# The turned tokens of a fused attention and feed-forward kernel: made per token half instead of per block of channels

## The reference, cut to what matters

```python
x = L0_attn_x                                        # (16, 512, 256)
x = _layernorm(x + _L0_attn_ref(x, Wqkv, bqkv, Wout, bout))
x = _layernorm(x + _L0_ffn_ref(x, ...))

def _tlin(x, w, s):
    return jnp.einsum('bsi,oi->bso', x, w) * s
h = jax.nn.silu(_tlin(x, w1_w, w1_s)) * _tlin(x, w2_w, w2_s)     # 256 -> 1024
h = jax.nn.gelu(_tlin(h, h1_w, h1_s), approximate=False)         # 1024 -> 1024
h = jax.nn.gelu(_tlin(h, h2_w, h2_s), approximate=False)         # 1024 -> 1024
return _tlin(h, w3_w, w3_s)                                      # 1024 -> 256
```

## Time and profile before

| | |
|---|---|
| median of three executions | 2168.33 us |
| span of the profiled execution (first to last instruction) | 2166.8 us |
| PE busy | 2118.4 us, 98% |
| ACT busy | 1316.1 us, 61% |
| DVE busy | 1259.9 us, 58% |
| POOL busy | 492.9 us, 23% |
| mean granted PE clock | 0.991 of full speed |

### The profile page before, as it was taken

The page is one execution under the profiler, slowest core; times in us unless marked ns, Lnnn a source line. Parts: engine busy times, 40 slices in busy tenths (PEclk is TensorE's granted clock), DMA queues, the critical chain, the costliest instruction groups (busy, mean ns, idle before and its releaser), DMA issues.

```text
span 2166.8 us, 52048 instructions
## 1 busy us (share of the span) xinstructions
PE 2118.4 (98%) x16294; PEld 1878.8 (87%) x16294; DVE 1259.9 (58%) x3928; ACT 1316.1 (61%) x2807; POOL 492.9 (23%) x899
## 2 busy tenths in 40 slices
PE   8789999999999999999999999999999999999998
PEld 4368889989889888899989889988999898988998
DVE  7765555556555565556556565565556556565452
ACT  6456566666556666566666666666566666656553
POOL 2222122221222222122221122222122132122220
PEclk9889999999999999999999999999999999999999
DMA  8742332232322332332232322333232232321100
GB/s 275 239 120 63 77 71 70 61 81 64 90 65 61 82 74 69 75 69 73 61 81 64 90 64 62 81 76 73 71 76 70 56 82 69 83 64 37 37 6 10
DMA packets 95940, 167.69 MB, mean 77 GB/s; under 512 B 19204, under 2 KB 38404, under 8 KB 95672
## 3 DMA queue, kind: packets, MB, share of 16 engines
q1 hardware_dynamic: 91912, 152.75, 28.6%
q10 hardware_dynamic: 3760, 11.54, 1.5%
HBM read 98.26 MB, written 68.17 MB: 77 GB/s over the span
## 4 chain that ended last, share of the span: by engine, by line
PE 89%; DVE 1%; DMA 0%; issue 0%; SPq 0%; ACT 0%; POOL 0%; POOLq 0%; DVEq 0%
PE ring L1241 44%; PE ring L1226 10%; PE pM L1116 7%; PE pS L1104 6%; PE pO L1164 6%; PE ring L1254 5%; PE ring L1176 4%; PE ring L1206 2%; PE ring L1196 2%; PE ring L1148 1%; PE ring L1215 1%; DMA qk_d<-c 0%; SPq L614 0%; DVE full_g L960 0%; DMA Qs<-nm 0%
## 5 line engine op out<-in xcount | busy, mean ns | idle before, releaser
L921 DVE CUSTOM_DVE_ANT_0 pM<-pM,mask 128x512 f32<-128x512 f32 (+3 forms) x1024 | 498.7, 502 | 366.1 <-PE pM L1116 292.3
L1241 PE MATMUL ring<-Yhi,H 128*128 128x256 f32 x1984 | 501.7, 289 | 0.0
L1241 PE MATMUL ring<-Xhi,H 128*128 128x256 f32 x1984 | 497.9, 288 | 0.0
L1241 PE MATMUL ring<-Ylo,H 128*128 128x256 f32 x1984 | 489.2, 282 | 0.0
L1241 PE MATMUL ring<-Xlo,H 128*128 128x256 f32 x1984 | 486.4, 282 | 0.0
L1241 PEld LDWEIGHTS ring<-Ylo,H 128*128 128x128 f32 x1984 | 377.8, 190 | 7.2 <-issue 3.4
L1241 PEld LDWEIGHTS ring<-Yhi,H 128*128 128x128 f32 x1984 | 377.0, 190 | 7.1 <-issue 3.4
L1241 PEld LDWEIGHTS ring<-Xlo,H 128*128 128x128 f32 x1984 | 379.1, 191 | 0.8
L1241 PEld LDWEIGHTS ring<-Xhi,H 128*128 128x128 f32 x1984 | 378.4, 191 | 1.0 <-issue 0.2
L1116 PE MATMUL pM<-Ks,Qs 128*128 128x512 f32 x992 | 304.2, 340 | 20.6 <-DVE mx L921 9.0
L865 ACT ACTIVATE Yhi<-ring,cols 128x256 fp32r<-128x256 f32 x248 | 117.8, 475 | 266.8 <-PE ring L1241 170.1
(11 more groups left out here) (146 smaller groups left out, 3518.7 us busy)
## 6 DMA issues: line engine op xcount, KB each, us to landing
qk_d<-c SPq DMA_DIRECT2D x120, 256.0 KB, 3.4
Qs<-qk_d SPq DMA_DIRECT2D x120, 192.0 KB
Ks<-qk_d SPq DMA_DIRECT2D x120, 192.0 KB
qk_d<-c SPq DMA_DIRECT2D x120, 128.0 KB, 3.0
xTs<-in_xT SPq DMA_DIRECT2D x16, 512.0 KB, 4.3
raw<-in_h SPq DMA_DIRECT2D x8, 1024.0 KB, 10.4
xz<-in_x SPq DMA_DIRECT2D x16, 512.0 KB, 3.9
H<-raw ACTq DMA_DIRECT2D x8, 1024.0 KB, 9.3
```

The lines of the kernel that those rows point to most:

```text
L921: nc.vector.tensor_tensor_reduce(pM[:, h % 2, 0:n], pM[:, h % 2, 0:n], mask[:, T - n:T], 1.0, NEG, ALU.add, ALU.max, mx[:, t, h:h + 1]).th ...
L1241: mm = nc.tensor.matmul(to, w, x_part, start=(k == 0 and m == 0), stop=(k == KB - 1 and m == 1))
```

## The change

A turn now makes one token half for both channel blocks: the argument of `x1_turn` is the half. The four transposes go into one bank as (channel block, token), ACT copies the whole bank into an `x1Thi` of half the size, and DVE fills an `x1Tlo` of half the size. The second half's turn overwrites the first half's buffers, so ACT waits until the first half's gate and up products have read them, and the turn stands behind them: in `ORDER` and `FIRST_ORDER` ahead of `ffn_out:-1:0:0`, in `TAIL_ORDER` right ahead of `gu:-1:1:0`, and in `HEAD_ORDER` no longer at all. The freed space is held by a placeholder tensor, so all other addresses stay.

```diff
-ffn_out:-2:1:0 x1_turn:-1:1 exp:0:1:0 exp:0:1:1 ffn_out:-2:1:1 exp:0:1:2 max:0:2:3:2 exp:0:1:3 gu:-1:0:0
+ffn_out:-2:1:0 exp:0:1:0 exp:0:1:1 ffn_out:-2:1:1 exp:0:1:2 max:0:2:3:2 exp:0:1:3 gu:-1:0:0
...
-h2:-1:0:7:1 max:1:0:3:0 qk:1:1 ffn_out:-1:0:0 table:0:Exp:6 exp:0:3:0 max:1:0:3:1 exp:0:3:1 stack:1:1
+h2:-1:0:7:1 max:1:0:3:0 qk:1:1 x1_turn:-1:1 ffn_out:-1:0:0 table:0:Exp:6 exp:0:3:0 max:1:0:3:1 exp:0:3:1 stack:1:1
...
-ffn_hi:-1:0:5 gu:-1:0:7 ffn_hi:-1:0:6 gu:-1:1:0 ffn_hi:-1:0:7 gu:-1:1:1 ffn_hi:-1:1:0 gu:-1:1:2 ffn_hi:-1:1:1
+ffn_hi:-1:0:5 gu:-1:0:7 ffn_hi:-1:0:6 x1_turn:-1:1 gu:-1:1:0 ffn_hi:-1:0:7 gu:-1:1:1 ffn_hi:-1:1:0 gu:-1:1:2 ffn_hi:-1:1:1
...
-        x1Thi = sb("x1Thi", [P, CB, T], F32R)
-        x1Tlo = sb("x1Tlo", [P, CB, T], F32R)
+        x1Thi = sb("x1Thi", [P, CB, HALF], F32R)
+        x1Tlo = sb("x1Tlo", [P, CB, HALF], F32R)
+        ctx.enter_context(nc.sbuf_tensor("x1_room", [P, CB, T], F32))
...
-                        c, = a
-                        act.wait_ge(xt_ready, b * CB + c + 1)
+                        half, = a
+                        act.wait_ge(xt_ready, b * 2 + half + 1)
...
-                        need(act, gu_ready, b * (2 * KB))
-                        nc.scalar.activation(x1Thi[:, c], ring[:, BANKS[kind, off, a]], ACT.Copy).then_inc(x1_hi, 1)
+                        need(act, gu_ready, b * (2 * KB) + half * KB)
+                        nc.scalar.activation(x1Thi[:].rearrange("p c n -> p (c n)"), ring[:, BANKS[kind, off, a]], ACT.Copy).then_inc(x1_hi, 1)
...
-                        for t in range(TB):
-                            mm = nc.tensor.transpose(to[:, t * P:(t + 1) * P], xz[:, (odd + off) % 2, t, c * P:(c + 1) * P], ident[:].bitcast(F32))
+                        for c in range(CB):
+                            for t in range(2):
+                                at = c * HALF + t * P
+                                mm = nc.tensor.transpose(to[:, at:at + P], xz[:, (odd + off) % 2, 2 * half + t, c * P:(c + 1) * P],
+                                                         ident[:].bitcast(F32))
...
-                        pe.wait_ge(x1_lo, (b + 1) * CB)
-                        tok = slice(half * HALF, (half + 1) * HALF)
+                        pe.wait_ge(x1_lo, b * 2 + half + 1)
```

More of the change, by code:

```diff
@@ L129 @@
 max:1:1:0:2 max:1:1:0:3 weights:0:10 pv:1:0:1 neg_split:1:1 weight_test:0:10 neg_max:1:1 ln1:0 low_bits:0 qk:1:3
-exp:1:1:0 exp:1:1:1 x1_turn:0:0 exp:1:1:2 x1_turn:0:1 max:1:2:3:0 exp:1:1:3 exp:1:1:4 o_out:1:0 weight_flag:0
+exp:1:1:0 exp:1:1:1 x1_turn:0:0 exp:1:1:2 max:1:2:3:0 exp:1:1:3 exp:1:1:4 o_out:1:0 weight_flag:0
 """
@@ L150 @@
 load_x:0 max:0:3:0:3 h_act:-1:h2:0:6 h2:-1:0:6:1 h_rest:-1:h2:0:5 neg_split:0:3 h2:-1:0:7:0 neg_max:0:3
-h_rest:-1:h2:0:6 h2:-1:0:7:1 h_rest:-1:h2:0:7 h_act:-1:h2:0:7 max:1:0:3:0 qk:1:1 ffn_out:-1:0:0 table:0:Exp:6
+h_rest:-1:h2:0:6 h2:-1:0:7:1 h_rest:-1:h2:0:7 h_act:-1:h2:0:7 max:1:0:3:0 qk:1:1 x1_turn:-1:1 ffn_out:-1:0:0 table:0:Exp:6
 ffn_out:-1:0:1 exp:0:3:0 exp:0:3:1 max:1:0:3:1 gu:-1:1:0 gu:-1:1:1 exp:0:3:2 ffn_hi:-1:1:0 exp:0:3:3 max:1:0:3:2
@@ L161 @@
 h_act:-2:h2:1:4 h_rest:-2:h2:1:4 x1_turn:-1:0 h2:-2:1:5:0 h2:-2:1:5:1 h_act:-2:h2:1:5 h_rest:-2:h2:1:5
-x1_turn:-1:1 h2:-2:1:6:0 h2:-2:1:6:1 h_act:-2:h2:1:6 h_rest:-2:h2:1:6 h2:-2:1:7:0 h2:-2:1:7:1 h_act:-2:h2:1:7
+h2:-2:1:6:0 h2:-2:1:6:1 h_act:-2:h2:1:6 h_rest:-2:h2:1:6 h2:-2:1:7:0 h2:-2:1:7:1 h_act:-2:h2:1:7
 h_rest:-2:h2:1:7 gu:-1:0:0 gu:-1:0:1 ffn_out:-2:1:0 ffn_hi:-1:0:0 ffn_out:-2:1:1 gu:-1:0:2 ffn_hi:-1:0:1
 gu:-1:0:3 ffn_hi:-1:0:2 gu:-1:0:4 ffn_hi:-1:0:3 ln2_stats:-2:1 gu:-1:0:5 ffn_hi:-1:0:4 ln2:-2:1 gu:-1:0:6
-ffn_hi:-1:0:5 gu:-1:0:7 ffn_hi:-1:0:6 gu:-1:1:0 ffn_hi:-1:0:7 gu:-1:1:1 ffn_hi:-1:1:0 gu:-1:1:2 ffn_hi:-1:1:1
+ffn_hi:-1:0:5 gu:-1:0:7 ffn_hi:-1:0:6 x1_turn:-1:1 gu:-1:1:0 ffn_hi:-1:0:7 gu:-1:1:1 ffn_hi:-1:1:0 gu:-1:1:2 ffn_hi:-1:1:1
 gu:-1:1:3 ffn_hi:-1:1:2 gu:-1:1:4 ffn_hi:-1:1:3 gu:-1:1:5 ffn_hi:-1:1:4 gu:-1:1:6 ffn_hi:-1:1:5 gu:-1:1:7
@@ L940, in work @@
                     elif kind == "x1_turn":
-                        c, = a
-                        dve.wait_ge(x1_hi, b * CB + c + 1)
+                        half, = a
+                        dve.wait_ge(x1_hi, b * 2 + half + 1)
                         if isinstance(b, int) and b == 0:
                             dve.wait_ge(*halves_used(2))
-                        nc.vector.tensor_tensor(x1Tlo[:, c], ring[:, BANKS[kind, off, a]], x1Thi[:, c].bitcast(F32),
+                        hi, lo = (part[:].rearrange("p c n -> p (c n)") for part in (x1Thi, x1Tlo))
+                        nc.vector.tensor_tensor(lo, ring[:, BANKS[kind, off, a]], hi.bitcast(F32),
                                                 ALU.subtract).then_inc(x1_lo, 1)
@@ L1047, in _ @@
                 "y": lambda half: (ln1, LN1, 2 * half + 1),
-                "x1_turn": lambda c: (x1_lo, CB, c + 1),
+                "x1_turn": lambda half: (x1_lo, 2, half + 1),
                 "neg_max": lambda g: (nm_done, NG, g + 1),
@@ L1224, in iteration @@
                                 for X in (x1Thi, x1Tlo):
-                                    w, x_part = parts(W[:, c, j * P:(j + 1) * P], X[:, c, tok])
+                                    w, x_part = parts(W[:, c, j * P:(j + 1) * P], X[:, c])
                                     mm = nc.tensor.matmul(to[:, n * HALF:(n + 1) * HALF], w, x_part,
```

## The result

The changed kernel takes 2173.51 us (median of 20 executions, 2170.53 to 2177.51), the kernel before 2168.23 us (20 executions, 2164.39 to 2172.49). The ratio is 1.0025, with a 95% interval of 1.0018 to 1.0031: slower by 5.3 us. The forecast was 2174.7 us.

What follows compares the result with a forecast made beforehand. PE, busy 98% of 2166.8 us, was taken as the bound. Terms 3.2+0.44-0.1-0.44-0.35+2.3 gave +5.0 at full clock, +6.4 with the clock's 1.4: 2174.7 us forecast, range 2170.0 to 2177.8.

Steps and rivals of the forecast that it cites:

- Old place, odd iterations: Group 1's first exp step, odd iterations from 5: PE arrives 0.44 us sooner, transfers do not; six times 0.44, 2.6 us.
- Old place, the others: Same exp step, remaining loop iterations: four with a small cushion lose together 0.54 us, four lose 0.
- Iteration 4: Behind the new place in iteration 4, PE's 0.76 us wait for full_g shrinks: -0.44 us.
- Iteration 16, the chain: Between the halves' gate and up products, rounding, copy and subtraction lie open: 2.71 us, +2.3 less the moved turn's 0.44.
- Iteration 16, the clock: Behind iteration 16's idle time the granted clock falls once, for a stretch of 3.41 us: 1.4 us.
- The head: Iteration 1's turn paid without gain, +0.44 us, and the head's flag copy perhaps sooner, -0.1 us.
- (a): Rival: the clock holds in the tail; +5.0, 2173.3 us; chance 0.24.
- (b): Rival: transfers land earlier, the loop costs nothing and only the tail is left; +1.8 at full clock, 2170.1 us; chance 0.19.
- (c): Rival: an earlier flag removes two low-clock stretches in the head; -1.0, or -4.2 with (b)'s loop, 2164.1 us; chance 0.05.
- (d): Rival: tail's clock falls two or three stretches, or all iterations land late; +9, 2177.5 us; chance 0.10 together with (e).
- (e): Rival: the second turn's copy stalls loop products, 14 times a piece of idle; chance within (d)'s 0.10.
- three signs I named for being wrong: Landings move with PE, transposes cost more behind the four-pass products, or the tail's idle time is under 2 us.

Runs made afterwards that it cites:

- Experiment 2: Changed kernel with the transposes of the first half's turn made twice: 2181.37 us, ratio 1.0056 to the kernel before.
- the split saves: Changed kernel, iteration 16 as before, two key saves of qk:0:3 behind group 1's nm transfers: 2167.41 us; kernel before with only that split: 2167.29 us.
- the form alone: Kernel before with turns per token half, two pairs of half-size buffers and all old orders: 2167.59 us, ratio 0.9999.
- the tail alone: Kernel before with only iteration 16 in the changed order, one pair of half buffers there: 2170.91 us, ratio 1.0013.
- the second busy tail: Changed kernel with needless matmuls in iteration 16, six ahead of the transposes' bank wait and eighteen behind the transposes: 2178.01 us, ratio 1.0036.
- the loop alone: Changed kernel's head, first iteration and loop, with iteration 16 as in the kernel before: 2172.45 us, ratio 1.0013.
- the two busy tails: Changed kernel with needless matmuls in iteration 16: sixteen behind the bank wait of gu:-1:1:0 (2174.74 us), or six and eighteen around the transposes (2178.01 us).
- the later saves: Changed kernel with all four saves of qk:0:3 on SP behind group 1's four nm transfers: 2179.94 us, ratio 1.0054.
- the filled tail: Changed kernel with split saves and first h1 steps between iteration 16's second turn and the second half's products: 2168.62 us, ratio 1.0001.

## Why the prediction was right, and where its terms were not

The sum was +6.4 on the profiled execution; the medians differ by 5.3, and the two profiles by 7.0. The two mechanisms that were to cost time both showed: PE comes sooner to a wait that does not move, and the open chain of iteration 16 with a fall of the clock behind it. The sizes of the terms were partly wrong. Term by term, from the two profiles:

- **Old place, odd iterations.** Predicted 0.44 for each. The iterations 5, 7, 9, 11 and 13 together take 651.15 us after 648.88: +2.27, where 2.2 was expected. In 15 the exp step stands 30.77 after group 0's, before 30.80: all 0.44 lost, as predicted. Experiment 2 shows that it is PE's arrival, and the split saves that it is the queue ahead of nm.
- **Old place, the others.** Predicted 0.54 for iterations 3, 8, 10 and 12. Iteration 3 lost 0.24, and the even ones nothing (6 to 14 take 129.47 to 129.49, 0.15 us less in all than before). This step failed in size: I read the cushion of each even iteration from one execution, and took a late end of SP there (1.37 in iteration 8, 1.98 in 6) for a property of the iteration. In the second profile of before the same distance is 1.95 in iteration 8 and 1.23 in iteration 12, which had 1.38. Hence seven waiting iterations and not the ten I named.
- **Iteration 4.** Predicted -0.44 of its wait of 0.76; the iteration got 1.29 us shorter. The kernel before, run again, has no such wait in iteration 4: I priced a chance event. Iterations made longer by such a wait turned up in four of the five profiles with the old loop order (iteration 4 before, 8 and 12 with the form alone, 8 with the tail alone and with the split saves) and in one of the nine with the new order (iteration 2 of the second busy tail: 130.32 us with a wait for full_g, 129.55 in the changed kernel). So the new order does not shut them out; whether it makes them rarer is open.
- **Iteration 2.** It got 0.31 shorter, where nothing was predicted. This is no chance: all five profiles with the old loop order have 129.87 to 129.89 there, and with the new order it is 129.54 to 129.56 in the five profiles in which nothing else lengthens it. In the kernel before, PE falls back by this much around a matmul of the max step at 322.40 (240.49 + 81.91), too little at a time to be listed as idle; in the changed kernel it doesn't. I had not compared iteration 2 with the others. Why the new order is free of it was not traced.
- **Behind iteration 15's start.** To `gu:-1:0:7` I had predicted -0.35 (+0.44 lost and -0.35 in iteration 15, -0.44 for the turn that leaves the h2 steps). It is -0.98. What I missed is a wait of before that the changed kernel does not have, in PE's timeline of iteration 15:

```profile
1970.73 0.36 PE L1226 MATMUL ring<-x1Thi,W 128*128 128x256 f32 x1 [0.70 <-DVE full_g L960]
```

  I had written that the loop shows no idle beyond iteration 4's, and iteration 15 is where that sentence was wrong. It repeats in the second profile of before (0.51 there) and is in none of those with the new loop order, so it was a term that could have been priced; its 0.70 is about the 0.63 that the sum missed.
- **Iteration 16, the chain.** Predicted +2.7 between the halves; 2.57 by the kernel in which the clock held. The transposes start at 2084.68 and the product at 2087.80, 3.12 later; I had 3.30 from the old product's start. The 0.18 between them: the copy starts 0.10 before the rounding's end (2086.44, 2086.54), and the product 0.06 behind the subtraction's end, where I had 0.15.
- **Iteration 16, the clock.** Predicted 1.4; measured 1.3 to 1.5. The Trainium skill, "TensorE: Matmul & The Clock Gate", in the section on HAM oscillation, warns only of long idle gaps; here the clock fell behind idle times of 0.90 and 2.49 us with four transposes between them. Where that section and these rows differ, the rows decide.
- **The head.** Predicted +0.3; the two profiles show +3.3. No run shows that this is a cost of the change. Heads with the new order and the same PE instructions took from 240.2 (the loop alone) to 246.6 us (the second busy tail) in eight profiles, heads with the old order from 239.4 (the form alone) to 242.6 (the split saves) in five. Their mean granted clocks differ, as PE's stretches show, before:

```profile
0.00:240.49 240.49, 205.23 (x1236) 0.92 0.54 164
```

  and after:

```profile
0.00:243.83 243.83, 207.44 (x1236) 0.90 0.54 162
```

By the clock's records the head before spent 37.5 us at the low clock and the one after 47.8. Eight profiles spent 41.0 us there: the two of them with the old order took 240.4 and 242.6 us, the six with the new order 240.2 to 242.1. So at equal time at the low clock the order makes no difference that shows. Whether it adds to that time is not settled: the five profiles with the old order have 34.1 to 41.0 us, the eight with the new order 41.0 to 51.2.

One pair of profiles is a poor check of the sum, so I also compare several. Four profiles with the old loop order and the saves in their old place have loops of 1685.7 to 1687.6 us (mean 1686.5), four with the new order (the changed kernel, the loop alone, the two busy tails) 1687.3 to 1688.0 (mean 1687.7): +1.3, where the sum had 3.2 - 0.44 - 0.44 = 2.3. This is the term that was too large: the even iterations lose nothing, and short waits of the old order, the one of iteration 2 and such as iteration 4's, are gone or rarer. For the tail the sum had 3.8 (0.44 - 0.35 + 2.3 + 1.4). Tails of before took 239.5 to 240.0 us in three profiles, those with the changed iteration 16 and no filler (the changed kernel, the tail alone, the later saves) 242.6 to 243.7: +3.4 between the means. Together that is 4.7, beside 5.3 between the medians with an interval of 3.9 to 6.7. The forecast was too high by 1.1 us of 6.4, and part of the agreement that is left is luck: the loop's term was nearly twice what it should have been, and the head's part is not known to a microsecond.

**The rivals.** (a), a clock that holds, is out: it fell in all four profiles with the changed iteration 16 and nothing between the halves (the changed kernel, the tail alone, the transposes made twice, the later saves). (b), transfers that move with PE, is refuted for the odd iterations by experiment 2; in the even ones coming sooner did cost nothing, though not because transfers moved. (c), a faster head, did not happen. (d), late everywhere, is out by the even iterations, and the clock was low for one stretch in the tail, not for two or three; its time should have read 2177.3 (2168.3 + 9), not 2177.5. (e) is out by the waits: no product in the loop waits for x1Tlo. The three signs I named for being wrong did not show.

**Why the odd iterations are late.** The prediction took this as given. The loop's body is two iterations, and its end falls into the middle of the odd one. DVE's timeline in the changed kernel, iteration 5 and then iteration 6:

```profile
652.47 0.38 DVE L995 BATCH_NORM_AGGREGATE mv<-st 128x2 f32<-128x6 f32 x4 [0.68 <-issue]
...
781.80 0.38 DVE L995 BATCH_NORM_AGGREGATE mv<-st 128x2 f32<-128x6 f32 x4
```

In the 0.68 us stands the loop's branch (its line, L440, has a branch of DVE at 651.6 and five more, one in each odd iteration from 5 to 15). From group 0's exp on, this operation starts after 19.83 us in iteration 5 and after 19.06 in iteration 6, and the delay is handed on: ACT's part of `c` starts 21.63 after 21.24, the first save of `qk:0:3` on SP 23.78 after 22.97, the copy to nm 24.90 after 24.35, and the first of the four nm issues 26.3 after 25.5. The kernel before shows the same (0.69 us, 19.83 and 19.06). So the 0.8 us by which the transfers are late in odd iterations arise at the loop's end, and the saves that stand ahead of nm on SP pass them on; with the saves behind or split, nm begins after 25.5 in iteration 5 and 25.0 in iteration 6. That the one follows from the other is read from the order of the steps and the equal distances; no kernel was run with the loop's end elsewhere.

**What stays open.** Why the head's stretches at the low clock differ between executions, and whether the new order adds to them. Why iteration 2 is free of its delay in the new order.

## What to carry to other kernels

Before moving a short piece of work on the bounding engine, look at what arrives just behind it: an engine that comes sooner to a wait gains nothing, and the same piece pays in full where it is put down. When such a wait hangs on a queue that issues in order, put the few issues that are not urgent behind it, and as few as possible: two moved saves won 3 us of the loop, four moved saves cost 6. Read a cushion or a short wait from at least two executions before it is priced; what repeats is a term, what does not is scatter. In an unrolled loop, look for the copy that holds the loop's end: here the iterations from 5 on that hold it are the ones that waited.

## What the runs showed of the hardware that I had not expected

The granted clock fell to 0.50 behind quite different stretches: with 0.63 us busy of 3.41 in the changed kernel, and, with the filled tail, behind a stretch in which PE was busy half of the time and its idle times were 0.90 and 0.84 us:

```profile
2077.60:2081.01 3.41, 1.68 (x13) 1.00 0.14 47
2081.01:2084.42 3.41, 3.35 (x17) 0.51 0.10 34
```

while in the head it fell behind a stretch with 2.02 busy and held behind one with 1.93. And a filler that comes too late does harm: sixteen matmuls of 256 columns, which start 0.12 us apart at full clock, took 3.41 us.
